# Storing the inverse softmax sums of an attention kernel to DRAM in transposed order, straight from one value per partition

## The reference, cut to what matters

```python
q, k, v = jnp.einsum('bsx,xMnd->Mbnsd', x, qkv)
a = jnp.einsum('bnsd,bntd->bnst', q, k) * q.shape[-1] ** (-0.5)
bias = jnp.where(rel >= 0, cum[:, jnp.clip(rel, 0)], PAD)
a = jax.nn.softmax(a + bias, axis=-1)
mix = jnp.einsum('bnst,bntd->bnsd', a, v)
attn = jnp.einsum('bnsd,ndx->bsx', mix, out_w)
```

## Time and profile before

| | |
|---|---|
| median of 3 runs | 1164.18 us (1155.86 to 1171.62) |
| the profiled execution: its time, its span | 1157.7 us, 1156.0 us |
| mean granted TensorE clock | 0.99 of full |
| PE, DVE, ACT busy | 96%, 70%, 63% of the span |
| DMA queue of SP and ACT (q1) | 62.1% of 16 engines |

### The profile page before, as it was taken

One profiled execution on the slowest core, in us unless ns is written; L12 is line 12 of the kernel. 1 busy time (PEld: TensorE's weight loads), 2 busy tenths in 40 slices (PEclk: granted clock), 3 DMA queues, 4 the chain that ended last, 5 costly groups with the idle time before them and its releaser, 6 DMA issues.

```text
span 1156.0 us, 21563 instructions
## 1 busy us (share of the span) xinstructions
PE 1106.1 (96%) x6973; PEld 791.9 (69%) x6973; DVE 809.3 (70%) x2121; ACT 731.1 (63%) x1857; POOL 6.4 (1%) x15
## 2 busy tenths in 40 slices
PE   6899999999999999999999999999999999999994
PEld 3666666766677777676777676777666777767773
DVE  2666666666657777776778777778776778777756
ACT  3666667665656676675766676767666667667633
POOL 1000000000000000000000000000000000000000
PEclk9999999999999999999999999999999999999998
DMA  8856565675657666656577656676756666665710
GB/s 200 222 142 150 140 153 145 152 186 137 155 135 168 160 166 161 169 144 174 134 176 171 166 149 155 163 177 164 185 135 155 164 169 158 169 164 144 234 40 20
DMA packets 113005, 180.71 MB, mean 156 GB/s; under 512 B 13152, under 2 KB 69360, under 8 KB 112896
## 3 DMA queue, kind: packets, MB, share of 16 engines
q1 hardware_dynamic: 110736, 178.42, 62.1%
q10 hardware_dynamic: 2160, 0.92, 0.3%
HBM read 58.41 MB, written 20.22 MB: 68 GB/s over the span
## 4 chain that ended last, share of the span: by engine, by line
PE 84%; DVE 5%; DMA 4%; issue 3%; ACT 2%; SPq 2%; POOL 0%; DVEq 0%; ACTq 0%
PE ps_o L1018 22%; PE ps_rows L977 21%; PE ps_t L994 17%; PE ps_m L952 9%; PE ps_m L957 5%; PE ps_m L1034 4%; PE ps_o L994 3%; DMA stacks<-k_lo 2%; DVE pt L684 2%; PE ps_rows L1090 1%; SPq L300 1%; DVE prob L660 1%; DMA prob<-in_L_attn_x 1%; ACT pt L519 1%; DVE mix_sb L691 1%
## 5 line engine op out<-in xcount | busy, mean ns | idle before, releaser
L501 ACT ACTIVATE prob<-prob,low 128x128 f32<-128x128 f32 (+7 forms) x512 | 394.5, 772 | 111.9 <-DVE low L660 106.0
L660 DVE CUSTOM_DVE_ANT_0 prob<-ps_rows,table 128x128 f32<-128x128 f32 (+7 forms) x512 | 379.9, 750 | 52.8 <-PE ps_rows L977 33.9
L977 PE MATMUL ps_rows<-stacks 128*128 128x512 f32 (+3 forms) x1536 | 401.1, 372 | 10.7 <-DMA stacks<-k_lo 6.1
L994 PE MATMUL ps_t<-ident,prob 128*128 128x128 f32 x1984 | 311.4, 278 | 6.4 <-ACT pt L519 3.5
L994 PEld LDWEIGHTS ps_t<-ident,prob 128*128 128x128 f32 x1984 | 231.4, 141 | 90.3 <-issue 74.6
L1018 PE MATMUL ps_o<-pt,v_pair 128*64 128x512 f32 (+3 forms) x1536 | 270.1, 494 | 0.0
L977 PEld LDWEIGHTS ps_rows<-stacks 128*128 128x128 f32 x1536 | 246.1, 190 | 32.0 <-DMA stacks<-k_lo 7.0
L684 DVE COPY pt<-ps_t 128x256 f32<-128x256 f32 (+2 forms) x320 | 178.2, 565 | 124.8 <-PE ps_t L994 124.2
L1018 PEld LDWEIGHTS ps_o<-pt,v_pair 128*64 128x64 f32 x1536 | 102.2, 137 | 177.5 <-issue 165.2
L519 ACT ACTIVATE pt<-ps_t 128x512 f32<-128x512 f32 (+3 forms) x352 | 162.8, 463 | 95.9 <-PE ps_t L994 95.6
L952 PE MATMUL ps_m<-x_cur,w_cur 128*128 128x512 f32 x250 | 131.6, 608 | 5.2 <-DVE q_lo L646 2.0
(11 more groups left out here) (118 smaller groups left out, 607.2 us busy)
## 6 DMA issues: line engine op xcount, KB each, us to landing
stacks<-k_hi SPq DMA_DIRECT2D x126, 256.0 KB, 4.6
stacks<-k_lo SPq DMA_DIRECT2D x126, 256.0 KB, 5.1
inv_all<-inverse_sums SPq DMA_DIRECT2D x128, 128.0 KB, 3.3
stacks<-q_hi SPq DMA_DIRECT2D x63, 256.0 KB, 4.0
stacks<-q_lo SPq DMA_DIRECT2D x63, 256.0 KB, 4.3
mix_transposed<-mix_sb SPq DMA_DIRECT2D x62, 256.0 KB, 3.8
table<-bias_by_distance SPq DMA_DIRECT2D x64, 192.0 KB, 3.6
mix_tile<-mix_transposed SPq DMA_DIRECT2D x24, 512.0 KB, 4.7
```

Of the source, the lines that this page charges most:

```text
L501: nc.scalar.activation(row, row, ACT.Exp, bias=low[:, r:r + 1], scale=-1.0, accum_out=total[:, r:r + 1]).then_inc(s_exp, 1)
L660: nc.vector.tensor_tensor_reduce(prob[:, r % PSLOTS, 0:width], ps_rows[:, score_at(r):score_at(r) + width], table[n % 2][:, h, 0:width][:, ...
L977: ins = nc.tensor.matmul(ps_rows[:, at + c0:at + c1], q_st(h, n)[:, P * i:P * i + P], k_st(h, n, low_part)[:, c0:c1], start=(low_part == 0 ...
L994: ins = nc.tensor.transpose(t_bank[TBANK[k]][:, P * b:P * b + P], prob[:, r % PSLOTS, at:at + P], ident[:, :])
```

## The change

The reciprocals are stored from `inv` itself. The DMA's DRAM side is written in the order "partition, then row": each partition's 8 values go to 8 places that are 512 B apart. The result in `inv_d` is the same. The two transposes of each step, the two copies into `inv_t`, the `inv_t` tiles and their semaphores are gone. The store waits for the reciprocal (`s_inv`) instead of for the copy, and the reciprocal now waits until the last step's store of the same group has landed (`s_inv_d`), instead of for the last step's transpose.

```diff
             def store_inverse(n, g):
 
-                sp.wait_ge(s_inv_t[g], n + 1)
-                sp.dma_start(inv_d[n % 2, g, :, :], inv_t[g][:, :]).then_inc(s_inv_d[g], 16)
+                sp.wait_ge(s_inv, 2 * n + g + 1)
+                sp.dma_start(inv_d[n % 2, g, :, :].rearrange("r q -> q r"),
+                             inv[:, 2 * GROUP * g:2 * GROUP * (g + 1)],
+                             allow_slow_non_contiguous=True).then_inc(s_inv_d[g], 16)
...
-                if k == INV_BANK[1]:
-                    if n > 0:
-                        act.wait_ge(s_inv_d[1], 16 * n)
-                    nc.scalar.activation(inv_t[1][:, :], t_bank[TBANK[k]][0:2 * GROUP, 3 * P:], ACT.Copy).then_inc(s_inv_t[1], 1)
...
                 dve.wait_ge(s_exp, NROWS * n + 2 * GROUP * (g + 1))
                 if n > 0:
-                    dve.wait_ge(s_tr, NBANKS * n + INV_BANK[g] + 1)
+                    dve.wait_ge(s_inv_d[g], 16 * n)
                 nc.vector.reciprocal(inv[:, rows], total[:, rows]).then_inc(s_inv, 1)
...
-                if k == INV_BANK[0]:
-                    if n > 0:
-                        dve.wait_ge(s_inv_d[0], 16 * n)
-                    nc.vector.tensor_copy(inv_t[0][:, :], t_bank[TBANK[k]][0:2 * GROUP, 3 * P:]).then_inc(s_inv_t[0], 1)
...
-                    if k in INV_BANK:
-                        g = INV_BANK.index(k)
-                        pe.wait_ge(s_inv, 2 * n + g + 1)
-                        ins = nc.tensor.transpose(t_bank[TBANK[k]][0:2 * GROUP, 3 * P:],
-                                                  inv[:, 2 * GROUP * g:2 * GROUP * (g + 1)], ident[:, :])
```

More of the change, by code:

```diff
@@ L90 @@
 INV_READY = (4, 13)
-INV_BANK = (5, 21)
 def build(nc, x, qkv, out_w, rpe, w_r, w_k, w_v, mu_r, mu_k, out):
@@ L136, in build @@
         inv = sb("inv", [P, NROWS])
-        inv_t = [sb(f"inv_t{g}", [2 * GROUP, P]) for g in range(2)]
         inv_all = [sb(f"inv_all{g}", [P, GROUP * P]) for g in range(2)]
@@ L211, in build @@
         s_inv = sem("inverted")
-        s_inv_t = [sem(f"inverse_transposed{g}") for g in range(2)]
         s_inv_d = [sem(f"inverse_in_dram{g}") for g in range(2)]
```

## The result

The changed kernel takes 1440.62 us (median of 6 runs, 1435.87 to 1445.24) against 1160.13 us for the kernel before (median of 6). The ratio is 1.2407, its 95% interval 1.2344 to 1.2471. The forecast was 1162 us and its range ended at 1220: the kernel is slower by a quarter.

The account below looks back on a forecast made before the run. PE, busy 96% of the span, was taken as the bound. -7.0 us for the transposes plus 4.6 us for group 0's slower store made -2.4 us, from 1164.2 to about 1162 us; range 1151 to 1220.

Parts of the forecast that it names:

- Part 1 and 2: Dropping 64 transposes takes 7.0 us off PE; dropping the copies on DVE and ACT was taken as 0.
- Part 3: On DVE, the reciprocal's wait for the last step's store of the same group to land; cost 0.
- Part 5: Group 0's store on SP: 64 pieces at 25 ns hold the spread back 0.8 us, costing 4.6 us in all.
- My upper bound: Price of a 4-byte piece in group 0's store, from the loads of `mu`: 0.22 us, 14 us for 64.
- The prediction's own formula: Loss from group 0's late store: 31e - 24 us, with e = 64c - 0.8 and c the price of a piece.
- The costly rival: Group 0's store lands late at over 40 ns a piece; 1226 us at 60 ns; chance 0.33.
- Part 4: Group 1's store on SP: landing a few us later is swallowed by SP's 6.3 us wait before q; cost 0.
- The signs: SP's spread waits 3 us and more each time, and PE's waits for the stacks grow from 4 to 31.

Follow-up runs that it names:

- the store in natural order: The change with the inverses stored partition then row, 128 pieces of 32 bytes, so the mix is scaled wrongly: 1150.47 us, ratio 0.9947 to the kernel before.
- the last version: The change with DVE transposing the inverses in 32x32 squares in SBUF, stored as 128 pieces of 128 bytes: 1148.12 us, ratio 0.9919 to the kernel before.

## Why the prediction was wrong

*Part 1 and 2, the transposes and copies: right.* 7.0 us were forecast for PE; the store in natural order gave 7.3, with an interval that the forecast lies in, and a step of the last version lasts 33.8 us, the number the prediction named. Part 3, the reciprocal's new wait, cost nothing that any profile shows.

*Part 5, the price of a piece: the step that failed.* "I take 25 ns, since that row has the count and the DRAM side." For pieces that stand apart this was right: alone, 1024 of them took 1.3 us more than 8 rows (20 ns each of 64), and in the kernel they gave 1155 us. But the row was a load, and its pieces were 512 bytes long. The new store's pieces are short writes side by side in DRAM, and they took 9.1 us more than the 8 rows: 0.14 us for each of 64. My upper bound was 0.22 us, and the measured price lies inside it; I set it aside as "most of which must be the other loads", and ended the range at 60 ns. The prediction's own formula, taken at its own upper bound of 14 us, gives 385 us lost and 1542 us; a range that took in this bound would have held the measured time.

*The costly rival: right in its place and its kind.* Its formula, 31e - 24, with e = 64 x 0.14 - 0.8 = 8.2 us, gives 230 us lost and 223 net, 1387 us. Measured are 1440. It even named neighbours whose writes meet. It had a chance of 0.33 and should have had more, or an end further out. The Trainium skill (DMA: Bandwidth & Descriptors, Specifications) has transfers under 512 B done as read-modify-write, and the prediction could put no price on it for want of a row. Being under 512 B isn't what costs here: 1024 pieces of 64 B side by side land after 2.1 us, and 4-byte pieces 64 bytes apart in transposed order after 2.6. Only short writes that lie close together show the cost, and whether a read-modify-write is behind it no run shows.

*What the formula lacked: the clock.* It let PE go on at full speed after each wait. The rows show 0.50 of the clock behind the stand. PE is busy for 64 us more than before, and for 74 us more than the 1096.1 us that the same matmuls take with the store in natural order. On the median of before, the rival's 230 us of waits and these 64 (the 7 us of the transposes are already off them) give 1164 + 294 = 1458, near the measured time, but not by getting each term right: in the profile the waits for k grew by 200 us, not 230. No part of the prediction costed what an idle PE does to PE.

*Part 4, group 1 at no cost: wrong.* Its slow store alone costs 63 us. The argument was that SP's spare time of 6.3 us in a step takes up a late landing. It does so for a few us; the landing was later by 8 to 9, the tables behind it landed late too, and two thirds of the spare time were gone, in 8 of the 31 steps all of it. With a landing as late as the forecast's own (1.6 us) it held: the kernel with the pieces 64 bytes apart still has 184.2 us of spare wait in 31 steps.

*The signs* named for the costly case, 3 us and more of wait in each step and 31 waits of PE for the stacks, are what the profile shows: 5.6 us each in 63 waits of both groups, and 35.

## What to carry to other kernels

A transposed store to DRAM with single values side by side isn't priced by its bytes or its count of pieces, but by how close together its short writes lie. Distance alone is a poor guide to what is safe: 32 bytes were enough when neighbours came from different partitions, and not when they came from one. Make the pieces 32 contiguous bytes at least (2.1 us for 1024, 1.4 us for 128), or transpose in SBUF first. When an unknown price sits behind an in-order queue with under 1 us of room, the range must reach to its upper bound, whatever the likeliest value. If PE would be made to wait, add the slower clock that follows the wait.

## What the runs showed of the hardware

- 1024 writes of 4 bytes to DRAM, alone, land after 10.3 us as neighbours; with neighbours from different partitions after 4.4 us at a distance of 8 bytes, 2.7 at 32 and 2.6 at 64; with neighbours from one partition after 5.7, 4.6 and 3.5 us at the same distances. Pieces of 32 bytes side by side take 2.1 us. The same 4-byte pieces into SBUF take 2.3 us, and read from DRAM 2.2 us.
- While such a store is pending, the DMA engines are almost idle (share 0.15, 7 GB/s), and two of them at once take 10.7 to 11.0 us, hardly longer than one. But DMAs issued within 0.5 us behind it land about when it does, on another queue (7.4 to 9.9 us for 1.2 to 1.3) and within SBUF too (8.2 us for 2.8).
- After PE had stood idle for the 4.65 us before 833.40, the granted clock was 0.50 for the next 3.6 us, 0.91 for 4 us and then 1.00.
- DVE transposes 128x32 float32 in squares of 32 in 0.21 us.
